# Routed experts of a recurrent and mixture-of-experts layer: the up projections with weights in the array and tokens streaming, in pieces of 192 to 384 places

## The reference

```
x  : 8 x 1024 x 512, float32 (8192 tokens of 512)
xn = layernorm(x)
s  = out projection of a gated recurrence over each sequence, from xn
topk = argmax(xn @ gate_w)                 # one of 32 experts
shared = (silu(xn @ sg) * (xn @ su)) @ sd  # inner size 1024
xs = xn * sigmoid(top logit)
g  = xs @ routed_gate_w[expert]            # 512 x 1024 each
u  = xs @ routed_up_w[expert]              # 512 x 1024
routed = (silu(g) * u) @ routed_down_w[expert]   # 1024 x 512
out = x + s * silu(shared + routed)
```

## Time and profile before

| | us |
|---|---|
| median of 3 runs (4074.55 to 4076.37) | 4075.29 |
| the profiled execution: time | 4077.65 |
| the profiled execution: span of its instructions | 4076.0 |
| shared stage, up to about | 1030 |
| recurrence stage, up to about | 2606 |
| routed stage | the rest |

### The profile page before, as it was taken

The page is one execution under the profiler, slowest core; times in us unless marked ns, Lnnn a source line. Parts: engine busy times, 40 slices in busy tenths (PEclk is TensorE's granted clock), DMA queues, the critical chain, the costliest instruction groups (busy, mean ns, idle before and its releaser), DMA issues. The chain is left out here.

```text
span 4076.0 us, 51548 instructions
## 1 busy us (share of the span) xinstructions
PE 3984.7 (98%) x17849; PEld 3230.3 (79%) x17852; DVE 1983.8 (49%) x2711; ACT 2003.6 (49%) x2512; POOL 834.1 (20%) x927
## 2 busy tenths in 40 slices
PE   7999999999989999999999999799999999999998
PEld 6888888888867888888888888588888888888886
DVE  4232323233345555555555555455656556565564
ACT  3222222222247766766676666454545455554552
POOL 2011110101014100000000000043434434444443
PEclk9999999999989999999999999899999999999999
DMA  4122121212121000110000010455657557566562
GB/s 164 65 78 77 74 80 72 82 51 90 44 81 44 32 32 31 51 42 31 31 31 31 34 59 10 151 196 190 213 173 255 196 190 258 200 229 216 191 229 87
DMA packets 197850, 447.44 MB, mean 110 GB/s; under 512 B 19737, under 2 KB 36313, under 8 KB 193954
## 3 DMA queue, kind: packets, MB, share of 16 engines
q1 hardware_dynamic: 165170, 346.24, 24.0%
q0 software_dynamic: 32624, 100.47, 7.2%
HBM read 345.90 MB, written 104.68 MB: 111 GB/s over the span
## 5 line engine op out<-in xcount | busy, mean ns | idle before, releaser
L82 PE MATMUL gate<-xT,w_hi 128*128 128x512 f32 x1536 | 601.4, 392 | 1.1 <-DVE b2all L952 1.1
L83 PE MATMUL gate<-xT,w_hi 128*128 128x512 f32 x1536 | 601.4, 392 | 0.0
L84 PE MATMUL gate<-xT,w_lo 128*128 128x512 f32 x1536 | 599.6, 390 | 0.0
L1162 DVE TENSOR_TENSOR wlo<-raw,whi 128x2048 fp32r<-128x2048 f32 x192 | 438.7, 2285 | 83.5 <-ACT whi L1158 83.5
L1367 PE MATMUL tY<-whi,thT 128*128 128x512 f32 x1264 | 426.5, 408 | 0.0
L518 DVE TENSOR_TENSOR h_act<-h_act,psU 128x512 f32<-128x512 f32 x128 | 87.9, 687 | 685.8 <-PE psU L84 685.7
L1158 ACT ACTIVATE whi<-raw 128x2048 fp32r<-128x2048 f32 x192 | 367.3, 1913 | 42.1 <-DMA raw<-in_L_ffn_routed_gate_w 17.0
L82 PEld LDWEIGHTS gate<-xT,w_hi 128*128 128x128 f32 x1536 | 288.8, 188 | 66.2 <-DVE b2all L952 2.6
L84 PEld LDWEIGHTS gate<-xT,w_lo 128*128 128x128 f32 x1536 | 289.1, 188 | 62.1
L83 PEld LDWEIGHTS gate<-xT,w_hi 128*128 128x128 f32 x1536 | 288.8, 188 | 60.2
L966 DVE SCALAR_TENSOR_TENSOR log_f<-gate,b1s,log_f 128x512 f32<-128x512 f32 x128 | 96.2, 751 | 420.4 <-ACT log_f L893 420.4
(11 more groups left out here) (187 smaller groups left out, 8454.4 us busy)
## 6 DMA issues: line engine op xcount, KB each, us to landing
raw<-in_L_ffn_routed_gate_w SPq DMA_DIRECT2D x64, 1024.0 KB, 6.5
raw<-in_L_ffn_routed_up_w SPq DMA_DIRECT2D x64, 1024.0 KB, 6.3
raw<-in_L_ffn_routed_down_w SPq DMA_DIRECT2D x64, 1024.0 KB, 6.9
xT_dram<-xT SPq DMA_DIRECT2D x16, 2048.0 KB, 6.3
xT<-xT_dram SPq DMA_DIRECT2D x14, 2048.0 KB, 7.9
x_in<-in_L_attn_x SPq DMA_DIRECT2D x16, 1024.0 KB, 5.4
xs_dram<-x_in SPq DMA_DIRECT2D x16, 1024.0 KB, 4.4
ss_dram<-y_sb SPq DMA_DIRECT2D x64, 256.0 KB, 2.1
```

Source lines behind the costliest of these rows:

```text
L82: pe.matmul(out, w[0], x[0], start=start, stop=False)
L83: pe.matmul(out, w[0], x[1], start=False, stop=False)
L84: return pe.matmul(out, w[1], x[0], start=False, stop=stop)
L1162: dve.tensor_tensor(wlo[q][:], raw[q][:], whi[q][:], ALU.subtract).then_inc(wlo_done[q], 1)
```

## The change

Only the routed stage changes, and the arithmetic that plans it. The up products are turned round. For each block b of 128 inner columns, 128 x 128 of gate weight stands in TensorE, and the expert's tokens, N of them, stream past; the same with the up weight: for each piece 8 blocks x 2 x 12 products of N columns. g, u and h then have the inner columns on partitions, which is what the down products need as their stationary operand, so h is not turned any more: ACT and DVE split it from SBUF. The down products stay as they were, 24 of 512 columns for each group of up to 128 places, the last group with only the rows it has.

An expert's tokens lie in pieces: as many full ones of 384 places as it takes, and a last one of 192 to 384, by 32. A plan of five rows (first piece, first unit of 32, first third group, number of full pieces, units of the last piece) takes the place of `first_tile`. The size of a piece must be known in the code, so each engine has one body for the full piece, in a loop, and seven for the last piece, chosen by a tree of branches (`by_size`); POOL has only its scatters in seven versions. The first 31 experts run in a loop and expert 31 is a separate copy, as before.

The weights still come in six parts of 1 MB, now four of two blocks of gate and up each, and two of down, and three raw buffers in a ring serve them: part q waits until the part three before it is split. Each part is loaded by two DMAs. Each piece turns three groups of 128 rows of x whatever its size, and gathers three of xg, ss and xr.

```diff
+UNIT = 32
+PIECE = 384
+LEAST = 192
...
+FIRST_PIECE, FIRST_UNIT, FIRST_THIRD, FULL, LAST = range(5)
...
-        xT = k.sb("txT", [P, 2, KD, P], F32R)
+        xT = k.sb("txT", [P, 2, KD, PIECE], F32R)
...
+        def by_size(eng, n, least, most, body):
+
+            if least == most:
+                return body(least)
+            half = (least + most) // 2
+            with eng.If(n > half):
+                by_size(eng, n, half + 1, most, body)
+            with eng.Else():
+                by_size(eng, n, least, half, body)
+
+        def experts(eng, piece):
...
             def expert(e, split):
-                t0 = eng.value_load(starts[0:1, bass.ds(e, 1)], min_val=0, max_val=NS - 1)
-                t1 = eng.value_load(starts[0:1, bass.ds(e + 1, 1)], min_val=1, max_val=NS)
-                with eng.If(t1 > t0 + 1):
-                    tile(t0, e, False)
...
+                p = order(eng, FIRST_PIECE, e, 0, E + MOST)
+                full = order(eng, FULL, e, 0, MOST)
+                n = order(eng, LAST, e, LEAST // UNIT, PIECE // UNIT)
+                with eng.If(full > 0):
+                    with eng.Fori(0, MOST) as i:
+                        with eng.If(full > i):
+                            piece(p + i, e, PIECE // UNIT, False)
+                by_size(eng, n, LEAST // UNIT, PIECE // UNIT, lambda size: piece(p + full, e, size, split))
...
             with sp.Fori(1, E) as e:
                 for q in range(PARTS):
-                    sp.wait_ge(wlo_done[q], e)
-                    sp.dma_start(raw[q][:], part(q, e)).then_inc(raw_loaded[q], 16)
+                    if q < RING:
+                        sp.wait_ge(wlo_done[q + RING], e)
+                    else:
+                        sp.wait_ge(wlo_done[q - RING], e + 1)
+                    load_part(sp, q, e)
...
+                for b in range(NI):
+                    silu(b)
+                    h_hi(b)
+                    if b % 2 == 1 and b < NI - 1:
+                        hi(b // 2)
+                act.wait_ge(u_mm, p * NI + NI)
+                x_hi(p + 1, 0)
+                hi(NQ - 1)
+                for g in range(1, GROUPS):
+                    x_hi(p + 1, g)
+                hi(D0)
...
+                for b in range(NI):
+                    h_mul(b)
+                    h_lo(b)
+                    if b % 2 == 1 and b < NI - 1:
+                        lo(b // 2)
+                x_lo(p + 1, 0)
+                lo(NQ - 1)
+                for g in range(1, GROUPS):
+                    x_lo(p + 1, g)
...
+                def up(b, m, bank, done):
+                    q, cols = b // 2, slice(b % 2 * P, b % 2 * P + P)
                     for kb in range(KD):
-                        mm = matmul_pairs(pe, bank[:], (xT[:, 0, kb, :], xT[:, 1, kb, :]),
-                                          (whi[q][:, kb, :], wlo[q][:, kb, :]), kb == 0, kb == KD - 1)
-                    mm.then_inc(used[q], 1)
+                        mm = matmul_pairs(pe, bank[b % 2][:, 0:N],
+                                          [pair(w[q][:])[:, m, kb, cols] for w in (whi, wlo)],
+                                          [xT[:, a, kb, 0:N] for a in range(2)], kb == 0, kb == KD - 1)
+                    mm.then_inc(done, 1)
...
+                for b in range(NI):
+                    if b % 2 == 0:
+                        pe.wait_ge(wlo_done[b // 2], e + 1)
+                    pe.wait_ge(sg_done, p * NI + b + 1)
+                    up(b, 0, psG, g_mm)
+                    pe.wait_ge(h_done, p * NI + b + 1)
+                    up(b, 1, psU, u_mm)
+                turn_x(p + 1, 0)
...
+                for g in range(GROUPS):
+                    if g > 0:
+                        turn_x(p + 1, g)
+                    if g < len(groups(n)):
+                        pe.wait_ge(z_done[g], p + 1)
+                        mm = down(0, *groups(n)[g])
...
+                for g, rows in groups(n):
+                    down(1, g, rows).then_inc(y_mm[g], 1)
```

More of the change, by code:

```diff
@@ new lines, in routed_sweep, with order, unit @@
+        out_stored = [k.sem(f"out_stored{g}") for g in range(GROUPS)]
+        block = ctx.enter_context(nc.Block())
+        def order(eng, what, e, least, most):
+            return eng.value_load(orders[0:1, what, bass.ds(e, 1)], min_val=least, max_val=most)
+        def unit(u):
+            return nc.s_assert_within(u, 0, NU, skip_runtime_bounds_check_because="the units of all experts are NU at most")
+        def by_size(eng, n, least, most, body):
[6 more added lines that the diff above has]
+                by_size(eng, n, least, half, body)
@@ L1205, in _ @@
-            fetch(yo[:], x_rows, at_next[:], out_stored)
-            pool.wait_ge(out_stored, 16)
-            experts(pool, tile)
-            total = pool.value_load(starts[0:1, E:E + 1], min_val=1, max_val=NS)
-            pool.wait_ge(xg_loaded, (total + 2) * 16)
-            settle(pool, settled)
-            pool.wait_ge(out_stored, (total + 1) * 16)
+                for g in range(GROUPS):
+                    fetch(ss[g][:], ss_dram, index(at_s, g), ss_loaded[g])
+                    fetch(xr[g][:], x_rows, index(at_s, g), xr_loaded[g])
@@ new lines, in _ @@
+            with pool.Fori(0, E - 1) as e:
+                expert(e)
+            total, third, n = expert(E - 1)
+            for g in range(GROUPS):
+                pool.wait_ge(xg_loaded[g], (total + 1) * 16)
+            for g in range(2):
+                pool.wait_ge(out_stored[g], (total + 1) * 16)
+            settle(pool, settled)
+            with pool.If(n > 2 * STEP):
+                pool.wait_ge(out_stored[2], (third + 2) * 16)
+                settle(pool, settled)
+            pool.wait_ge(out_stored[2], (third + 1) * 16)
@@ L1258, in tile @@
+                if len(groups(n)) < GROUPS:
+                    act.sem_inc(zs_done[2], 1)
                 hi(D1)
-            experts(act, tile)
+            experts(act, piece)
         @block.vector
         def _(dve):
-            for n in range(2):
-                dve.sem_inc(h_done[n], 1)
-                dve.sem_inc(hlo[n], 1)
-            dve.sem_inc(z_done, 1)
-            dve.sem_inc(zm_done, 1)
-            def x_lo(t):
-                dve.wait_ge(xhi, t + 1)
-                dve.tensor_tensor(xT[:, 1], psX[:], xT[:, 0], ALU.subtract).then_inc(xlo, 1)
@@ L1394, in moe_recurrent_kernel @@
+            experts(pe, piece)
 def moe_recurrent_kernel(nc, x, W1, b1, W2, b2, init_h, gate_w, sgw, suw, sdw, rgw, ruw, rdw, out):
```

505 lines of the change are left out of this document (283 added, 222 removed).

## The result

| | us |
|---|---|
| before, median (4074.6 to 4076.4) | 4075.3 |
| after, median of 4 runs (4717.5 to 4726.9) | 4719.7 |
| ratio, 95% interval | 1.158 [1.156, 1.160] |
| the profiled execution of after, span | 4715.8 |
| forecast | 4320, range 3950 to 4450 |

The change makes the kernel 15.8% slower. The direction was the likelier one of the forecast, the size is outside its range. The first two stages take the same time as before; all of it lies in the routed stage.

The account below looks back on a forecast made before the run. TensorE's own products bound the routed stage. Own work 1260 + start 20 + chain waits 26 + switches 307 + lower clock 75 = 1688 us instead of 1441, so 4076.0 + 247 = 4323, say 4320; range 3950 to 4450.

Parts of the forecast that it names:

- TensorE's own work: Routed stage: up and down products and turnings fall from 1396 to 1260 us.
- start: Start of the routed stage: waits in the first tile, 8.3 us and more, kept at 20 us.
- Up products: Gate and up products: N columns cost N/2.4 + 13.5 ns, at least 0.110 us; 861 us falls to 786.
- Rival 4: Products under 512 columns stream slower, 0.19 us at 224 places; with free code 4072 us, no change; chance 0.06.
- Down products, turnings: Down products stay at 430 us; turnings of h go, 70 us; turnings of x rise by 8 us.
- The chain of ACT and DVE: Behind up products, second turning of x waits for DVE: 1.5 us an expert, 47 in all; 26 with PE late.
- The switch: Between experts: three of five far jumps miss code at 3.6 us; 9.9 us idle each, 307 us over 31.
- The clock: After idle at each expert switch, 5.6 us at half speed lose 2.4 us, 75 us over 31.
- beside PE's wait; I add nothing: At expert switches ACT and DVE jump through eight bodies too, alongside PE's wait; nothing added.
- Rival 1: Expert loop's code comes free, kept or covered by queued products: 3970 us, bounds 3940 to 4060; chance 0.36.
- Rival 3: At expert switches all far jumps miss, or ACT's and DVE's misses line up with PE's: 4450 to 4560; chance 0.07.

Follow-up runs that it names:

- the three bodies: Changed kernel with only three last-piece bodies (256, 320, 384 places) and no full-piece body on PE, ACT and DVE: 4068.5 us, ratio 0.9980.
- three sizes: Changed kernel with bodies of 256, 288 and 352 places, no full-piece body, and steps of ACT and DVE moved, weight splits included: 3987.0 us, ratio 0.9780.
- a jump over 6.6 blocks: Kernel before, with ten more tile bodies on PE behind a condition that never holds: 4077.3 us, ratio 1.0001.
- 8.4 with an unused body: Changed kernel with last-piece bodies of 256, 320 and 384 places, the never-run full-piece body left in: 4427.6 us; with that body on PE alone 4308.7 us.
- 8.4 that all run: Changed kernel with four last-piece bodies (256, 288, 320, 352 places) and no full-piece body: 4278.4 us, ratio 1.0492.
- two moves: On the 4068.5 us kernel (256, 320, 384 places): x rounding and part 5's split moved, 4063.4 us; then fewer plan loads, earlier output add, later split, 4049.5 us.

## Why the prediction was wrong

The terms of its sum, against the distances of successive starts in the stage of after. What a product takes above its full-clock distance, and below three times of it, is counted as clock; what a first product at a turning or a block takes above it, as a wait.

| us | forecast | after |
|---|---|---|
| TensorE's own work (up, down, turnings) | 1260 | 1266 |
| start | 20 | 21 |
| waits for ACT and DVE inside pieces | 26 | 36 |
| idle at 31 switches | 307 | 698 |
| products at the lower clock | 75 | 69 |
| stage | 1688 | 2090 |

The two stages are not cut alike: the forecast's 1688 stands against 1441 from the first up product on, the 2090 begin with the turning of the slot table at 2609.7, from where the kernel before took 1450. So the stage grew by 640 us where the forecast had 247, and 391 of the 393 us between them are the row of the switches. The row of the start agrees by luck. The forecast's 20 were waits for data in the first tile; after's 21 are one more wait for code, three branches of 6.3, 5.2 and 6.5 us ahead of the first product.

- **Up products: right.** In the timeline a product of 192 places takes 0.112 us, of 224 0.113, of 256 0.120, of 288 0.133, of 320 0.147, of 352 0.160. The form N/2.4 + 13.5 ns and the floor of 0.110 held to within 0.003, and 384 places came out at 0.173 by the same form. Rival 4 is refuted. In the timeline of after, twelve products of 192 places from 3667.35 to 3668.69, 1.34 us:

```profile
3667.35 0.28 PE L86 MATMUL tG<-txT,whi 128*128 128x192 f32 x1
...
3668.69 0.28 PE L86 MATMUL tU<-txT,whi 128*128 128x192 f32 x1
```

- **Down products, turnings: right**, to within the sum's 6 us.
- **The chain of ACT and DVE: right in after, mis-sized behind it.** With PE late it cost 36 us for 26. Where PE is not late, in the three bodies, it was 3.5 us in the mean expert of 256 places and not 1.5: 61 us for 31 experts and 12 more in the first, where the forecast had 47. The forecast saw only the second turning. The wait for the first silu, behind DVE's second output, three register loads and a table load in line, was not in it.
- **The switch: the step that failed.** Its mechanism was right: PE waits for code at far jumps, and the queue q8, the idle time ahead of the first tG and the clock digits show it where the prediction said they would. Both factors of its 307 us were too small; the measured 698 are the miss. It took three of five jumps as missing; 4.7 branches an expert are long. It took 3.6 us for one, from the only cold jump of before; the mean is 5.1. One block was fetched at that jump, 2.5 in the mean here: the 52 branches within which one block's transfer starts last 4.3 us (median), the 93 with two 5.2. 4.7 x 5.1 = 24 us of branches, less the 3.9 us in the queue, plus the 3.0 of registers give the 23 that the switches have. At the forecast's two numbers this was 9.9. The price was taken from one jump that queued products hid in part, so that only two releases of the sequencer bounded it, and it should have been a lower bound.
- **The clock: right, by luck in its parts.** The granted clock of 0.82 in the stretch counts the idle time too. After 26.9 us of idle, products of 320 places stand 0.267 us apart from 3506.54 to 3508.67, the lower level of 1.2 GHz, and 0.147 from 3509.3 on: 3 us at half speed and about 1.4 lost, where the earlier trace rows had shown 5.6 us and 2.4. By the single records, 50 of the 69 us stand behind the 31 switches, 1.6 each where the forecast had 2.4; the other 19 stand elsewhere and were not in the term.
- **ACT and DVE "beside PE's wait; I add nothing": right for the sum only.** They lie beside it because PE's wait is the longer one, not because theirs is short: alone they cost 326 us, which stay when only PE's code is made to fit.
- **Rival 1 (code for free, 3970 us)** was a real case: with code that fits and the waits moved, three sizes give 3987, and seven would have 26 us less to compute. Against its chance of 0.36 stood a loop of 17 blocks with none longer than 6 known to stay. **Rival 3** named what happened (all far jumps miss), and its price, again with 3.6 us for a jump, ended at 4560.

One reading of the prediction was off without effect: the mean in the earlier trace rows is 395 ns, not 392.

The rule of the Trainium skill ("Runtime: NRT & Kernel Launch", Instruction fetch mechanics) that a branch out of the current two blocks waits for a fetch would have given 4545 as an estimate, nearer than the forecast. The runs don't bear it out as it stands. The loop of three bodies spans 6.3 blocks and fetches 19 in all from 2665 on, in 31 experts, and a jump over 6.6 blocks was free. Its other statement, 128 KiB held, which is 8 blocks, fits better: 6.3 blocks stay but for 7 long branches (31 us), 8.4 miss in part, 17 miss at most jumps. It does not explain why 8.4 with an unused body miss more than 8.4 that all run.

## What to carry to other kernels

Count the instructions of a loop that chooses among unrolled bodies, on every engine and with the bodies that never run, before counting what the better fitting body saves: here the limit lay between 6.3 and 8.4 blocks of PE's code and between three and four bodies on ACT and DVE, and beyond it a far jump of PE cost 5 us. Three sizes keep 49 of the 75 us that seven would save on the up products, and the whole gain on the turnings. When a step is moved to take a wait away, ask first which buffer the late engine holds: here reading the PSUM bank before a long step starts was worth 53 us on top of two moves that had brought 19.

## What the runs showed of the hardware

- In the changed kernel a branch of PE to code that is not at hand lasts 3.3 to 7.6 us, median 5.0, with 2.5 blocks of 16 KiB fetched in the mean; one at hand lasts 0.07 to 0.25.
- The other engines' code comes over another queue (q14) in blocks of 8 KiB. 28 of them were fetched with three bodies on ACT and DVE, 180 with four, 395 with seven, 426 with eight (the unused full piece's counted). ACT stood still for 12.8 us at one switch.
- An unused body of 2.2 blocks ahead of three that run cost 240 us on PE, while ten unused bodies (6.6 blocks) in one stretch beside 2.0 blocks that run cost nothing. What decides between these two is open.
- Products of this kind follow N/2.4 + 13.5 ns from 512 columns down to 256 (0.227 and 0.120 us) and stay at 0.112 to 0.113 for 224 and 192. The distance of two weight loads in the earlier trace rows was 0.11 us too; that the load sets this floor fits it, and no run separates the two.
